# Polynomial attention: state from scaled keys, one projection for all groups, half of the diagonal's weights on GpSimd

## What is computed

```
att = einsum('bhid,bhjd->bhij', q, k) / sqrt(8), causal
w   = (s**2 + 1 if s > 0, 1 - s / 100 from -100 to 0, else 0) / 1000   for each score s
y   = einsum('bhij,bhjd->bhid', w, v)
out = x + y.reshape(B, T, C) @ W_proj
```

## Time and profile before

| | us |
|---|---|
| three timed runs, median (lowest to highest) | 3188.33 (3187.82 to 3189.63) |
| the profiled execution, its own time | 3197.16 |
| its span in the profile | 3195.43 |
| its mean granted TensorE clock | 0.919 of full |
| PE busy, of the span | 2832.2 (89%) |
| DVE busy | 2087.3 (65%) |
| ACT busy | 1199.9 (38%) |
| POOL busy | 836.7 (26%) |

### The profile page before, as it was taken

How to read it: one execution, slowest core, us unless ns; L and a number is a source line. 1 busy time by engine, 2 the same in 40 slices (tenths; PEclk the granted TensorE clock), 3 DMA queues, 4 the chain that set the end, 5 groups by cost and what they waited for, 6 DMA issues and landing times. The chain is left out here.

```text
span 3195.4 us, 55424 instructions
## 1 busy us (share of the span) xinstructions
PE 2832.2 (89%) x15400; PEld 1924.1 (60%) x15400; DVE 2087.3 (65%) x5242; ACT 1199.9 (38%) x2164; POOL 836.7 (26%) x1220
## 2 busy tenths in 40 slices
PE   5999999958787888689999998869989989999986
PEld 4777777735555555467777776445465465465453
DVE  6777777747676777577777776355556556555533
ACT  2111111127565657521111111335545545545532
POOL 1222332225555555423222332001101101111100
PEclk8999999958888788899999998879999999999988
DMA  3000000000000000110000000000000000000000
GB/s 130 0 0 0 0 0 0 1 0 2 3 2 3 2 2 2 61 44 0 0 0 0 0 0 1 0 1 1 1 2 1 1 1 1 1 1 1 1 1 27
DMA packets 12996, 23.60 MB, mean 7 GB/s; under 512 B 2306, under 2 KB 7682, under 8 KB 12804
## 3 DMA queue, kind: packets, MB, share of 16 engines
q1 hardware_dynamic: 12804, 21.22, 2.0%
HBM read 18.52 MB, written 2.10 MB: 6 GB/s over the span
## 5 line engine op out<-in xcount | busy, mean ns | idle before, releaser
L555 DVE SCALAR_TENSOR_TENSOR moe_acc<-moe_ps,moe_comb,moe_acc 128x512 f32<-128x512 f32 x896 | 661.1, 744 | 174.5 <-PE moe_ps L304 167.9
L2017 DVE CUSTOM_DVE_ANT_0 attn_masked<-attn_psm,attn_causal 128x1024 f32<-128x1024 f32 (+7 forms) x512 | 367.6, 755 | 210.4 <-PE attn_psm L1742 199.3
L1921 ACT ACTIVATE attn_probs<-attn_pse 128x512 f32<-128x512 f32 (+1 forms) x640 | 319.9, 553 | 301.6 <-PE attn_pse L1756 301.0
L304 PE MATMUL moe_ps<-moe_Wg,moe_xh 128*128 128x512 f32 x1024 | 329.4, 403 | 25.0 <-DVE moe_Wu L501 25.0
L335 PE MATMUL moe_ps<-moe_Wd,moe_ih 128*128 128x512 f32 x1024 | 337.8, 411 | 0.0
L304 PE MATMUL moe_ps<-moe_Wu,moe_xh 128*128 128x512 f32 x1024 | 337.1, 411 | 0.0
L1772 PE MATMUL attn_psy<-attn_probs,attn_V 128*64 128x512 f32 (+3 forms) x1536 | 325.5, 524 | 0.3 <-POOL attn_probs L1677 0.3
L454 POOL TENSOR_SCALAR moe_part<-consts,moe_pick,moe_prob 128x8 f32<-128x8 f32 x256 | 98.1, 398 | 752.1 <-ACT moe_prob L389 752.1
L1677 POOL TENSOR_SCALAR_AFFINE_SELECT attn_probs<-attn_probs 128x256 f32<-128x256 f32 (+1 forms) x192 | 95.1, 495 | 757.7 <-ACT attn_probs L1921 757.7
L1021 POOL TENSOR_TENSOR attn_R<-attn_R 128x1024 f32<-128x1024 f32 (+1 forms) x128 | 215.5, 1690 | 201.6 <-DVE attn_R L1365 201.4
L1756 PE MATMUL attn_pse<-attn_qS,attn_kS 110*128 110x512 f32 (+3 forms) x768 | 233.2, 394 | 21.4 <-ACT attn_probs L1921 15.2
(11 more groups left out here) (208 smaller groups left out, 4871.2 us busy)
## 6 DMA issues: line engine op xcount, KB each, us to landing
moe_stageg<-in_w_gate SPq DMA_DIRECT2D x8, 512.0 KB, 7.2
moe_stageu<-in_w_up SPq DMA_DIRECT2D x8, 512.0 KB, 8.3
moe_stageg<-in_w_down SPq DMA_DIRECT2D x8, 512.0 KB, 3.7
out<-X SPq DMA_DIRECT2D x1, 2048.0 KB, 8.9
attn_qS<-attn_mh SPq DMA_DIRECT2D x64, 4.0 KB
attn_qS<-attn_ml SPq DMA_DIRECT2D x64, 4.0 KB
attn_wd<-in_wd SPq DMA_DIRECT2D x1, 864.0 KB, 5.7
attn_w<-in_wqkv SPq DMA_DIRECT2D x1, 768.0 KB, 5.1
```

The lines of the kernel that those rows point to most:

```text
L304: last = pe.matmul(expert_bank[j % 4][:, :], a[q][:, :], w[b][:, cols], start=k == 0, stop=k == 2)
L555: dve.scalar_tensor_tensor(acc[:, q, r, :], expert_bank[j % 4][:, :], comb[:, q, r, e:e + 1], acc[:, q, r, :], ALU.mult, ALU.add).then_inc ...
L1921: act.activation(probs[:, u % 2, c, HALF - n:HALF], e_bank[c][:, HALF - n:HALF], ACT.Exp, scale=SCORE_SCALE).then_inc(p_ready, 1)
L2017: dve.tensor_tensor_reduce(masked[:, k % 2, 0:n], m_all[:, base:base + n], causal[:, SEQ - n:SEQ], 1.0, NEG, ALU.add, ALU.max, mx[:, q, v: ...
```

## The change

1. The group of a weight matrix has four blocks of 128 columns instead of three (`GW`): query, key, key times the slope -0.01, value. `KV` is made from the last two, so the running sum comes out as the state needs it. POOL's `state` is gone, and with it `runm`, `runl` and `S`. There are two buffers `run`.
2. The state part is made head by head from `run` in plain fp32: for each chunk four products of 32 rows by 32 columns instead of one of 128 by 128.
3. Each group's values lie in columns of their own of a band (`V_FROM`, `V_TO`, `WINDOW`), so the groups' outputs can be added: ACT copies `y_bank` to `yS` for g = 0, and for g = 1 to 3 DVE adds it (`add_out`). The projection is one product for each tile of tokens, 8 instead of 32.
4. The diagonal weights of heads 0 and 1 are made on POOL by `tensor_scalar` and `tensor_tensor`; ACT and DVE keep those of heads 2 and 3.

The diff, cut to its core:

```diff
             @block.gpsimd
-                def state(m, q):
-                    pool.wait_ge(av_ready, after(m * NU + NU - 1))
...
-                    pool.tensor_tensor(S[q][:, :, :], runm[:, :, :], f32(runl[:, :, :]), ALU.subtract).then_inc(S_ready, 1)
+                def diagonal(m, g, u):
+                    r = R[:, slot(g % 2, u), 0:2, :]
+                    pool.wait_ge(pv_ready, after(m * NU + u - SLOTS))
+                    pool.wait_ge(read01, after(m * NU + u))
+                    pool.sem_inc(pool_pause, 1)
+                    pool.tensor_scalar(r, T0[:, 0:2, :], LIFT, -2.0 * LIFT, ALU.max, ALU.add).then_inc(xr_ready, 1)
+                    pool.wait_ge(xr_ready, after(m * ND + DIAGONAL.index(u)))
+                    pool.sem_inc(pool_pause, 1)
+                    pool.tensor_tensor(r, r, T0[:, 0:2, :], ALU.mult).then_inc(x01_ready, 1)
                 def step(m, g, b, more, has_next):
-                    for u in OTHERS:
-                        square(m, g, u)
+                    for u in range(1, NU):
+                        if u in DIAGONAL:
+                            diagonal(m, g, u)
+                        else:
+                            square(m, g, u)
                     if has_next:
-                        state(m + 1, (g + 1) % 2)
+                        diagonal(m + 1, (g + 1) % GROUPS, 0)
             @block.tensor
                 def values(m, g, u):
+                    if end:
+                        pe.wait_ge(av_ready, after(m * NU + NU - 1))
                     if u in DIAGONAL:
+                        pe.wait_ge(x01_ready, after(m * ND + DIAGONAL.index(u)))
                         pe.wait_ge(x_ready, after(m * ND + DIAGONAL.index(u)))
...
-                        pe.wait_ge(S_ready, after(m))
                         for c in chunks:
-                            last = pe.matmul(y_bank[:, (c % 4) * P:(c % 4 + 1) * P], S[q][:, c, :], qS[q][:, c * P:(c + 1) * P],
-                                             start=False, stop=c == chunks[-1], skip_group_check=True)
+                            for j in range(GH):
+                                rows = slice(j * ROW, (j + 1) * ROW)
+                                last = pe.matmul(y_bank[rows, (c % 4) * P:(c % 4 + 1) * P], run[q][rows, c, rows],
+                                                 f32(qS[q][rows, c * P:(c + 1) * P]), start=False, stop=c == chunks[-1],
+                                                 skip_group_check=True)
                 def finish(b, more):
                         for j in range(4):
-                            for g in range(GROUPS):
...
+                            c = s * HALF + j * P
+                            last = pe.matmul(e01[1][:, s, j * P:(j + 1) * P], yS[:, c:c + P], wp[:, :], start=True, stop=True)
             @block.scalar
                     if u in DIAGONAL:
-                        for h in range(2):
...
+                        act.wait_ge(read23, after(m * NU + u))
+                        act.activation(R[:, r, 2:4, :], T0[:, 2:4, :], ACT.Relu, bias=minus_lift).then_inc(rd_ready, 1)
                 def copy_out(m, g, s):
+                    if g == 0:
             @block.vector
                 def take(m, g, u):
                     if u in DIAGONAL:
+                        dve.wait_ge(x01_ready, after(m * ND + DIAGONAL.index(u) - 1))
                 def diagonal(m, g, u):
-                    for h in range(2):
...
+                    r = R[:, slot(g % 2, u), 2:4, :]
+                    dve.wait_ge(rd_ready, after(m * ND + DIAGONAL.index(u)))
+                    dve.scalar_tensor_tensor(r, r, -LIFT, T0[:, 2:4, :], ALU.add, ALU.mult).then_inc(x_ready, 1)
                 def step(m, g, b, more, has_next):
+                        if k == NQ0 + 1:
+                            add_out(m, g, 0)
...
+                    add_out(m, g, 1)
                     correct(dve, dve_pause, m, g % 2, lambda: low_weights(m, g), ((cc_ready, US), (cm_ready, 2 * ND), (cy_ready, 2)))
+                def add_out(m, g, s):
+                    if g:
+                        dve.wait_ge(y_ready, after(m * 2 + s))
+                        y = yS[:, s * HALF:(s + 1) * HALF]
+                        dve.scalar_tensor_tensor(y, y_bank[:, :], 1.0 / DIVISOR, y, ALU.mult, ALU.add).then_inc(yc_ready, 1)
```

More of the change, by code:

```diff
@@ L907, in attn0_phase @@
         qS = [sb(f"qS{q}", [P, SEQ], F32R) for q in range(2)]
[L908 to L912, removed]
+        KV = [sb(f"KV{q}", [P, BT, 2 * (P + q * WINDOW)]) for q in range(2)]
+        run = [sb(f"run{q}", [P, BT, P]) for q in range(2)]
         R = sb("R", [P, SLOTS, GH, HALF])
@@ L994, in _ @@
             def _(pool):
[L995 removed]
+                for s in (sq01_ready, xr_ready, x01_ready):
                     pool.sem_inc(s, LEAD)
[L997 removed]
+                for q in range(2):
+                    pool.memset(run[q][:, 0, :], 0.0).then_inc(zero_ready, 1)
                 pool.wait_ge(w_in, 48)
@@ L1466, in attn0_laid_out @@
 def attn0_laid_out(np, a, r):
-    wqkv = a["L0_attn_W_attn"].reshape(DIM, 3, GROUPS, GH, HD)
-    w = np.zeros((DIM, GROUPS, 3, GH, ROW), np.float32)
+    wqkv = a["L0_attn_W_attn"].reshape(DIM, 3, GROUPS, GH, HD).transpose(1, 0, 2, 3, 4)
+    w = np.zeros((DIM, GROUPS, 4, GH, ROW), np.float32)
     for part in range(3):
-        w[:, :, 0:2, :, part * HD:(part + 1) * HD] = wqkv[:, 0:2].transpose(0, 2, 1, 3, 4)
-    w[:, :, 2, :, 0:HD] = wqkv[:, 2]
+        rows = slice(part * HD, (part + 1) * HD)
+        w[:, :, 0, :, rows], w[:, :, 1, :, rows] = wqkv[0], wqkv[1]
+        if part < 2:
+            w[:, :, 2, :, rows] = wqkv[1]
@@ L1472, in attn0_laid_out @@
+    wp = np.zeros((GH, ROW, DIM), np.float32)
+    for g in range(GROUPS):
+        w[:, g, 3, :, V_FROM[g]:V_FROM[g] + HD] = wqkv[2][:, g]
+        wp[:, V_TO[g]:V_TO[g] + HD] = a["L0_attn_W_proj"].reshape(GROUPS, GH, HD, DIM)[g]
     r["wqkv"] = w.reshape(P, GROUPS * GW)
-    wp = np.zeros((GROUPS, GH, ROW, DIM), np.float32)
-    wp[:, :, 0:HD] = a["L0_attn_W_proj"].reshape(GROUPS, GH, HD, DIM)
-    r["wproj"] = wp.transpose(1, 2, 0, 3).reshape(P, GROUPS * DIM)
-    row, col = np.arange(P) % ROW, np.arange(P)
+    r["wproj"] = wp.reshape(P, DIM)
@@ L1484, in attn0_laid_out @@
     small[:, 4:8] = np.arange(P)[:, None] // ROW == np.arange(GH)
-    same = (np.arange(P)[:, None] // ROW) == (col[None, :] // ROW)
-    small[:, 8:136] = same * np.where(row < 24, SLOPE, np.where(row < 26, 1.0 - HALF_LIFT * HALF_LIFT, 0.0))[:, None]
-    small[:, 136:264] = ((row == 24) | (row == 25))[None, :]
-    small[:, 392:904] = np.tile(np.triu(np.ones((P, P))), (1, 4))
+    small[row == 24, 8], small[row == 25, 8], small[row == 26, 8] = lift_parts(np)
+    small[:, 9], small[:, 10] = -LIFT, HALF_LIFT
@@ L1489, in attn0_laid_out @@
+    small[:, 12:12 + P] = np.where(row == 24, 1.0 - HALF_LIFT * HALF_LIFT, 0.0)[None, :]
+    small[:, 12 + P:] = np.tile(np.triu(np.ones((P, P))), (1, 4))
     r["attn0_small"] = small
```

88 lines of the change are left out of this document (40 added, 48 removed).

## The result

| | before | changed |
|---|---|---|
| median, us | 3188.07 (4 runs) | 3232.19 (4 runs, 3232.03 to 3232.95) |
| profiled execution, us | 3197.16 | 3232.26 |
| its span, us | 3195.4 | 3230.5 |

The changed kernel is slower: ratio 1.0138, 95% interval 1.0120 to 1.0156, +44 us. The forecast was 3220 (+31.5), with a range of 3192 to 3243.

The account below looks back on a forecast made before the run. No engine was full; a full queue held PE's sequencer before its branch at each boundary. Terms 25.8 + 14.0 - 4.0 - 2.3 - 2.0 = +31.5 us gave 3220 us, range 3192 to 3243.

Parts of the forecast that it names:

- The branch: At 12 boundaries inside batch elements, PE's branch starts 2.8 us later behind the longer tail; net +2.15 each, +25.8 us.
- The relief of 0.65 from POOL's lock: At those 12 boundaries, later scores find DVE free of POOL's state, so 0.65 us of the delay comes back each time.
- The first halves: Where an item's first half ends, 16 times: more state products, DVE's add and the items that normalise; +14.0 us together.
- The add: DVE's add ahead of L1348 at the first half's end, for g above 0: 0.5 us uncovered, 12 times, +6.
- The three items that normalise: Items with g = 2 normalising at step 3, DVE late: the whole add and the lock count, +0.9 each, +2.7.
- the lock in unit 3: Rival: POOL's work delays DVE's remaining L1372 in unit 3 without cover; +16 on top, 3236 us; 4%.
- Batch ends: Three batch element ends: shorter projection gains 4.1 us, the later branch takes 2.8 back; -1.3 each, -4 in all.
- last end: End of the last batch element, where the branch was shorter and nothing follows: -2.3 us.
- start: Start of the stage: DVE's diagonal ends some 2.6 us earlier, wider weights cost 0.6; together -2 us.
- A deep queue: Rival: PE's queue takes the whole tail, so boundaries cost only 0.55 us each; +7 us, 3195; 12%.
- Faster by the lock: Rival: POOL's state holds DVE at each boundary and the branch hides the longer tail; -23.5 us, 3165; 12%.
- The cold clock: Rival: a longer gap stretches the half clock after each boundary by a further 3.4 us; +20 on top, 3240; 12%.

Follow-up runs that it names:

- e1: Changed kernel with the second half's constant and state part issued ahead of unit 7's values instead of behind unit 9's: 3192.83 us, ratio 1.0009.
- e5: Changed kernel with PE only waiting for the flag and counting up two semaphores, without the branch or its part in the correction: 3170.19 us, ratio 0.9948.
- e12: Changed kernel with an empty correction under PE's branch, both ways counting up the two semaphores: 3172.93 us, ratio 0.9954.
- e2: Changed kernel with the second half's state part as 4 products of 128 x 128 (8 records, not 32), masking by head left out: 3201.14 us, ratio 1.0039.
- e3: Changed kernel with DVE's add of the first half's output behind the maximum of the bound instead of ahead: 3223.85 us, ratio 1.0118.
- e11: Changed kernel with the first half's state part as 3 products of 128 x 128 (6 records, not 24), masking left out: 3228.87 us, ratio 1.0131.
- e4: Changed kernel with the diagonal weights of heads 0 and 1 made by ACT and DVE again, POOL only squaring: 3221.17 us, ratio 1.0110.
- e8: Changed kernel with POOL's first diagonal pass as one operation in unit 0 and a two-input sum in unit 3: 3231.06 us in one run.
- e9: Changed kernel with the diagonal back on ACT and DVE, the add behind the maximum, and the second half's tail spread over steps 6, 7, 8: 3170.92 us.
- e10: Kernel before with the second half's constant and state part cut in three and issued at steps 6, 7 and 8: 3192.23 us, ratio 1.0017.

## Why the forecast held, and where it didn't

*The branch, +25.8 forecast, +33.4 measured.* The step was right in kind, and e1, e5 and e12 show it: a queue that lets the sequencer go late, and a branch behind it. The signs came too: 3.87 us of issue (3.5 forecast), a projection of 2.67 us (2.3), DVE's remaining diagonal at 1.22 in the median (1.2 to 2.3). But the number is nearer than its terms.

- The place of line 965 moved by 2.99 us after items with g of 0 and 1 (2.8 forecast; 24 records were left, now 20 or 21) and in the last of the four items that follow one with g = 2. In the other three of these it moved by 4.8, 3.8 and 4.4. In two of them the granted clock was lower over the values and the tail (0.66 of full in the 7.3 us from 824.4, where it was 0.82 in the 5.2 us from 821.9 before); in the third it was the same (0.82 and 0.81) and the values began 0.66 us later. That is 3.3 in the mean, +39.9 in all against 33.6: the term that was mis-sized.
- The relief of 0.65 from POOL's lock (-7.8) hardly came. It could not come before the scores of unit 1, which follow the wait by 3.9 to 5.3 us before (mean 4.74) and 3.5 to 5.2 now (4.80), always right behind the branch. At step 2 to 3, where PE waits for `kS`, 2.3 us come back in all.
- In its place 6.3 us come back at step 1 to 2, in three items with g = 2, by something that the forecast doesn't have. There the kernel before stood still for issue one group behind the scores, 2.07, 2.07 and 2.41 us at the same place of the code in three batch elements, as e2 does elsewhere; the changed kernel doesn't:

```profile
947.09 1.64 PE L1052 MATMUL attn_a<-attn_xT,attn_w 128*128 128x512 f32 x3 [2.07 <-issue]
```

```profile
958.56 1.19 PE L1056 MATMUL attn_a<-attn_xT,attn_w 128*128 128x512 f32 x3
```

That this nearly stands in for the missing relief is luck: without it these boundaries would have cost +39.7.

*The first halves, +14.0 and +18.1.* The products, 0.33 by their groups, measured 0.33 in work and 0.5 in the step. The add, 0.5 forecast, measured 0.4; e3 shows that its place causes it. The three items that normalise were priced at 0.9 each and lost 2.5 in the mean (1.4 to 2.5 in the traces of e1, e2, e5, e11 and e12, which keep POOL's work and the add in place); this price was mis-sized. The loss is gone without POOL's diagonal (e4: -0.1, -0.2 and 0.4) and small with the add out of the way (e3). The length of POOL's pass, which I took for 1.21 to 1.90 from rows of other forms and which is 3.63, does not make it: e8, in its one trace, has the short pass and no smaller loss (2.9 in the mean). The length only decides what POOL's product holds, the normalise or DVE's diagonal in unit 3. So in the changed kernel the lock in unit 3 didn't come because the pass was longer than I thought, which is luck; in e8 it came, 2 us of it, and the 13 items that don't normalise lost no more at step 6 to 7 than in the changed kernel. The cover that I counted on is there.

The Trainium skill (GPSIMD Engine Reference, section 4.1) says that with one input GpSimd is roughly at VectorE's rate and with two about twice as slow. With one input the trace differs: POOL takes 2.76 and 3.63 us where VectorE's L1375 takes 1.22 for as many elements, over twice as long. With two it takes 1.89 (both the same) and 2.36 (two different ones), where VectorE's L1369 takes 1.22: 1.5 to 1.9 times as long, not far from the page.

*Batch ends -4.0, last end -2.3, start -2.0:* measured -3.2, -3.0 and -4.5.

*The rivals.* A deep queue is out: 15 to 24 records, with 15 to 20 loads, were left at every boundary between items in the kernels with a branch. Faster by the lock is out, since line 965 moved by 3 us and more. The cold clock as I had drawn it is out (0.56 against 0.57 after the boundary, and 3.8 us less in all from unit 3's scores to unit 5's); a little of it lies in the two boundaries above. The measured difference came 12.6 above the forecast one; 6.3 are in the stage's steps (37.8 against 31.5). The other 6.3 can't be placed: the two profiled executions differ by 35.1 and the medians by 44, so outside the stage the profiled pair even shows 2.7 less, and I leave this open.

*What the change is worth.* With the same spread of the tail, the changed kernel without POOL's diagonal (e9) is 21 us faster than the kernel before (e10). So the new state and the single projection together are worth having, though no run parts them; the place of the 40 records of the tail cost 39, the add's place up to 8, POOL's diagonal up to 11 (the last two overlap). That e9 could be joined with a short branch was not tried.
